# Second attention: the scores for the exponentials as whole matmuls of 128 keys by 256 queries, where they were four pieces of 32 keys by 160 queries

## What is computed

```
x = x + attn_a(layernorm(x));  x = x + ffn(layernorm(x))
x = x + attn_b(layernorm(x));  x = x + ffn(layernorm(x))

# attn_b, for each batch and head, q and k with rotary embedding:
scores = q @ k.T / sqrt(16)
rel = k_idx[None, :] - q_idx[:, None]
local_ok = (rel <= 0) & (rel >= -127)
allowed = (local_ok | (k_idx % 64 == 0) | (q_idx % 64 == 0)) & (rel <= 0)
out = softmax(where(allowed, scores, -1e9)) @ v
```

## Time and profile before

| | |
|---|---|
| time, median of 3 | 3148.17 us (3146.51 to 3150.44) |
| time of the profiled execution | 3137.59 us |
| its span, first to last instruction | 3135.9 us |
| mean granted TensorE clock | 0.967 of full |
| busy over the span | PE 94%, PEld 69%, DVE 84%, ACT 54%, POOL 41% |
| second attention, steady part | about 1961 to 2490 us of the span |

### The profile page before, as it was taken

How to read it: one execution, slowest core, us unless ns; L and a number is a source line. 1 busy time by engine, 2 the same in 40 slices (tenths; PEclk the granted TensorE clock), 3 DMA queues, 4 the chain that set the end, 5 groups by cost and what they waited for, 6 DMA issues and landing times. The chain is left out here.

```text
span 3135.9 us, 105499 instructions
## 1 busy us (share of the span) xinstructions
PE 2946.0 (94%) x41228; PEld 2161.9 (69%) x41260; DVE 2625.3 (84%) x5413; ACT 1697.9 (54%) x3301; POOL 1270.7 (41%) x1572
## 2 busy tenths in 40 slices
PE   6999999999999799999996994999999969999999
PEld 4556777777777377777774653878777647777776
DVE  5778999999999499999994993777777669999997
ACT  5646787778788533333333662666656623333333
POOL 3561222112222244444432882555555624444442
PEclk9998999999999899999998996999999979999999
DMA  6682444444443222222223665455555322222221
GB/s 209 219 242 61 100 104 99 99 95 95 95 98 81 73 84 86 87 88 86 87 66 106 219 213 143 127 143 139 141 139 137 95 85 88 83 89 88 84 89 52
DMA packets 362151, 353.88 MB, mean 113 GB/s; under 512 B 79066, under 2 KB 298714, under 8 KB 361642
## 3 DMA queue, kind: packets, MB, share of 16 engines
q1 hardware_dynamic: 357162, 347.56, 40.0%
q10 hardware_dynamic: 4608, 0.79, 0.1%
HBM read 211.37 MB, written 135.27 MB: 111 GB/s over the span
## 5 line engine op out<-in xcount | busy, mean ns | idle before, releaser
L948 DVE TENSOR_REDUCE aA_nmax<-bank 128x1 f32<-128x512 f32 (+3 forms) x1216 | 715.5, 655 | 59.8 <-PE bank L1008 53.5
L990 ACT ACTIVATE aA_prob<-bank 128x512 f32<-128x512 f32 (+1 forms) x1216 | 617.0, 581 | 153.5 <-PE bank L1008 148.2
L1008 PE MATMUL bank<-aA_qk 96*32 96x512 bf16 (+17 forms) x12288 | 654.5, 317 | 13.6 <-issue 6.5
L1008 PEld LDWEIGHTS bank<-aA_qk 99*32 99x32 bf16 (+1 forms) x12288 | 408.7, 96 | 176.9 <-issue 48.3
L933 POOL TENSOR_SCALAR_AFFINE_SELECT aA_prob<-aA_prob 128x512 f32<-128x512 f32 x256 | 160.9, 634 | 663.3 <-ACT aA_prob L990 663.3
L1008 PE MATMUL bank<-aA_prob,aA_vq 128*32 128x512 f32 (+3 forms) x3072 | 357.1, 490 | 0.9 <-POOL aA_prob L933 0.9
L1498 PE MATMUL bank<-aB_qk 96*32 96x160 bf16 (+4 forms) x9344 | 309.4, 230 | 31.6 <-POOL aB_og L1321 18.5
L1498 PEld LDWEIGHTS bank<-aB_qk 96*32 96x32 bf16 (+3 forms) x9344 | 243.1, 98 | 97.9 <-issue 34.4
L1468 ACT ACTIVATE aB_prob<-bank 128x512 f32<-128x512 f32 (+1 forms) x512 | 262.3, 575 | 81.8 <-PE bank L1498 77.9
L1375 DVE TENSOR_REDUCE aB_nnear<-bank 128x3 f32<-128x480 f32 (+1 forms) x352 | 207.8, 636 | 55.7 <-PE bank L1498 50.6
L1356 POOL TENSOR_SCALAR_AFFINE_SELECT aB_prob<-aB_prob 128x512 f32<-128x512 f32 x256 | 163.4, 638 | 194.1 <-ACT aB_prob L1468 192.5
(11 more groups left out here) (212 smaller groups left out, 6195.3 us busy)
## 6 DMA issues: line engine op xcount, KB each, us to landing
aA_qk<-parts_A SPq DMA_DIRECT2D x384, 128.0 KB, 3.9
aB_qk<-parts_B SPq DMA_DIRECT2D x384, 128.0 KB, 3.3
parts_A<-pA_part SPq DMA_DIRECT2D x96, 256.0 KB, 4.8
parts_B<-pB_part SPq DMA_DIRECT2D x96, 256.0 KB, 3.1
o_A<-aA_o_sb SPq DMA_DIRECT2D x32, 512.0 KB, 3.0
o_B<-aB_o_sb SPq DMA_DIRECT2D x32, 512.0 KB, 2.9
pA_xin<-x SPq DMA_DIRECT2D x16, 512.0 KB, 4.5
v_A<-pA_vs SPq DMA_DIRECT2D x16, 512.0 KB, 4.6
```

What stands on the lines that cost most here:

```text
L948: nc.vector.tensor_reduce(dst, src, AX.X, ALU.max, negate=True).then_inc(s["m_taken"], 1)
L990: nc.scalar.activation(dst, src, ACT.Exp, scale=SCALE).then_inc(s["e_taken"], 1)
L1008: return nc.tensor.matmul(out, lhsT, rhs, start=start, stop=True, skip_group_check=True)
```

## The change

In `exp_unit` on PE the inner loop over four pieces of 32 keys goes. Each of the two heads of a unit gets one matmul with all 128 keys as weights and all w queries streamed (w is 256, and 128 in the last key block, k = 7). Before, a piece streamed the 160 queries from its own first key on (at most w - 32j of them), and the rest of the bank kept what was in it. Every place that POOL leaves in has the same value as before.

```diff
                 for e in range(2):
-                    for j in range(4):
-                        t0, t1 = 32 * j, min(32 * j + SPAN, w)
-                        ins = mul(out[32 * j:32 * j + 32, e * w + t0:e * w + t1],
-                                  ks[g][0:KROWS + 3, h0 + e, k * P + 32 * j:k * P + 32 * j + 32],
-                                  qs[g][0:KROWS + 3, h0 + e, k * P + t0:k * P + t1], True)
+                    ins = mul(out[:, e * w:(e + 1) * w], ks[g][0:KROWS + 3, h0 + e, k * P:(k + 1) * P],
+                              qs[g][0:KROWS + 3, h0 + e, k * P:k * P + w], True)
             ins.then_inc(s["e_made"], 1)
```

## The result

| | median | range | runs |
|---|---|---|---|
| before | 3147.34 us | 3142.73 to 3150.44 | 4 |
| after | 3214.12 us | 3211.26 to 3217.31 | 4 |

The ratio is 1.0214, with a 95% interval of 1.0196 to 1.0231: 67 us slower. The forecast was 86 us slower, 3234 us, with a range of 3190 to 3270. The profiled execution after took 3217.31 us, with a span of 3215.6; the one before took 3137.59, so that the two profiles lie 80 us apart, 13 more than the medians.

A forecast was written before the change was run, and what follows sets the result against it. PE's matmuls were taken to bound the second attention. Streaming 35.8 plus passings 62.6, less 4 of issue gaps and 8 of waits, gave 86 us, added to 3148 for 3234 us; range 3190 to 3270.

The forecast's parts named there:

- the prediction's own bounds: Limits on the forecast from its streaming, passings, give-back, weights and roundings: 3211 to 3272 us.
- What bounds the kernel: Second attention's steady part: PE's matmuls are 95.0% of the chain, so added PE time lengthens the run almost one for one.
- Streaming: Score units on PE: whole matmuls stream 80 ns more in each of 448 units, 35.8 us; nothing for 64 units.
- Passing: Switching PE between pieces and whole matmuls: 0.10 us in, 0.115 out, 286 more pairs, 62.6 us.
- Weights hidden: Score units on PE: the second head's 128-column load hides behind streaming, the first head's lies in the passing; otherwise 16 us.
- What is given back: PE's gaps in the stage: 4 us of issue through fewer instructions, 8 us of waits through later PE.
- No drain: Rival, 8%: bf16 pieces and whole matmuls follow each other freely, leaving streaming less give-back, 24 us, 3172.
- Faster or the same: Rivals with cheap passings: faster, 4%, PE bound by instructions and waits, 3137 us; no difference, 3%, 3148 us.
- The clock: Part of a rival: a tenth of the stage falls to PE's lower clock, adding 55 us, 3289.
- The dearer passing: Part of a rival: a passing behind a whole matmul costs its full latency, 70 ns more, 20 us in all.
- the open weights: Part of a rival: weight loads in score units are not hidden, 16 us more; with costlier passings 3270.
- more than the sum: Rival, 10%: the granted clock falls, 3289 us, or drains hit harder and weights are not hidden, 3270 us.

The follow-up runs named there:

- e9: The kernel before with whole matmuls in the last key block alone (64 of 512 units); 3143.10 us, ratio 1.0015.
- e2: The kernel before with one whole matmul of 16 columns added ahead of each unit's pieces; 3212.93 us, ratio 1.0235.
- e3: The kernel after, each whole matmul streaming only the first 160 queries, so the output is incomplete; 3178.87 us, ratio 1.0122 against before.
- e6: The kernel before with the turning of the global probabilities and the global output in four pieces each; 3203.56 us, ratio 1.0200.
- e7: The kernel before with turning, global output and `far` unit all in pieces, no whole matmul left in the stage; 3270.43 us, ratio 1.0425.
- e4: The kernel before with two pieces of 64 keys by 192 queries in place of four of 32 by 160; 3208.19 us, ratio 1.0221.
- e5: The kernel before with each piece of a unit cut into two of half the columns; 3208.20 us, ratio 1.0227.
- e8: The kernel before with the global output alone in pieces, one a head; 3157.93 us, ratio 1.0058.
- e11: The kernel after with the turning and the global output in pieces; 3202.94 us, ratio 1.0206 against before.

## Why the prediction was right, point by point

**The number.** 86 us were forecast and 67 measured; 3214 lies 3 us above the lowest time that the prediction's own bounds allowed, 3211. Two terms of the sum were off, the passing and what is given back, and both made it too large; the streaming was a little too small.

**What bounds the kernel**: right. PE was the chain and is it now to 99.8%; ACT's wait for PE rose from 73.1 us to 125.8. The group of 17.1 us in the prediction is a stretch of PE without its gaps; the group took 18.0 us on average, and 20.4 after.

**Streaming, 35.8 us**: right for 448 units: pairs start 0.11 to 0.12 us apart, 0.109 of it columns. The other 64 were taken as nothing, and e9 shows some 5 us for them, 3 of it PE's own work, with the overlap of short pieces as the cause read from the trace.

**Passing, 0.219 us a pair, 62.6 us in all**: right in kind, 9% too dear. Measured 0.106 + 0.094 = 0.20. The step that was off is the duration of a whole matmul of 256 columns: from 16 columns I carried 195 ns up to 297, and it is 273 (a mean of 276 over all). The list counted to its end has 187 passings before, not 183; with 755 after that is 284 pairs and 56.8 us.

**Weights hidden**: right. The second matmul of a unit starts 0.12 us after the first, the first pair's extra 11 ns being part of the passing.

**What is given back, 12 us**: the term that was sized wrong. Some 22 us went, all that there was: 10 of issue and 12 of waits for ACT and its queue. The prediction had 14.8 us of issue, of which 4.6 were the missing record in rows 6, though it had named that record itself. And it gave a quarter of the issue gaps back because a quarter of the instructions goes; e2 has more instructions than before and no gap at all. They went because PE takes longer over the same stream, so that each packet of instructions is there in time. With the sizes measured the sum is 35.8 + 56.8 + 3 (the last block) - 22 = 74 us. That is what the stage grew by between the two profiles; the medians lie 67 apart, and where the other 7 us lie no run shows.

**The rivals.** No drain is out by e3 (+38 where it said nothing). Faster or the same would have needed passings below 19 and 30 ns; they are about 100. The clock did not move with the change (1.00 before and after); in e6 and e7, with gaps of a fifth of the chain, it did. The dearer passing and the open weights of "more than the sum" are out too: going out costs 0.094 us, and the second matmul of a unit starts on time.

**What stays open**: some 7 us of e4, how much of the loss of e6 and e7 is the clock's, and why a packet comes when it does.

## What to carry to other kernels

Before merging small matmuls into larger ones, look at their neighbours in the engine's list: each change between strip widths costs here 0.1 us in and 0.1 out, more than the 0.14 us that the whole unit took, and the pieces it replaces may stream fewer columns side by side. Read what a matmul costs from the distance between starts, and test a stream of instructions for supply (issue gaps inside a unit, without a semaphore, that end a fixed time after an instruction packet) before dividing work more finely, counting an f32 matmul twice as the trace does: a change that slows such an engine gets its gaps back, and one that quickens it may get nothing.

## What the runs showed of the hardware

- Pieces of one width stream side by side, four pieces of 160 columns in 0.07 us. A change of width (32, 64 or 128 columns) lets the next kind begin 0.07 us before the last matmul of the old one ends, whatever the types.
- PE with a load before each matmul never used more than about 30 of such pairs a microsecond over the stage (30.1 in e5, 29.7 in e7), with instruction packets of 16 KB each 4.2 us. Issue was 1.9% of the chain at 26.8 and none at 24 (e2), but 6.3% at 23.4 where dense stretches stand in it (e11).
- When PE runs out of instructions it starts again 1.2 to 1.8 us after the next packet has landed (385 gaps); a packet is 256 instructions, and no two started closer than 3.3 us.
- With issue gaps of 18.6 and 23.5% of the chain the granted clock was 0.93 on average (e6, e7), with 6.3 to 11.4% it was 0.98 (e5, e8, e11), in a stage where it was 1.00 before.
